# Setup of a fused attention and feed-forward kernel: early load of one bias, reordered setup work, and q_stack transfers split differently between SyncE and ScalarE

## What is computed

```python
xn = layernorm(x)
# attention block ("cosformer"): 16 heads of 16, causal, linear in L
q, k, v = split(rmsnorm(xn, n1) @ qkv_w + qkv_b)
q, k = relu(q), relu(k)                      # then times cos and sin of the position
context = q_cos * cumsum(k_cos x v) + q_sin * cumsum(k_sin x v)
norm    = q_cos . cumsum(k_cos) + q_sin . cumsum(k_sin)
h = xn + (context / (norm + 1e-6)) @ out_w + out_b
a = h + gelu(rmsnorm(h, n2) @ mlp_w1 + mlp_b1) @ mlp_w2 + mlp_b2
# second block: ternary weights, each row scaled by the mean of its absolute values
t = ternary(w_fc)    # clip(round(w / s), -1, 1) * s, s = mean(abs(w))
g = xn @ t.T + gate * (xn @ v.T @ fast_b.T @ u.T)
f = square(relu(g)) @ ternary(w_proj).T
out = x + a + f
```

## Time and profile before

| what | value |
|---|---|
| median of 3 runs | 640.94 us (640.76 to 641.73) |
| profiled execution, its own time | 644.8 us |
| its span, first to last instruction | 641.9 us |
| busy: PE, VectorE, ACT, POOL | 92%, 66%, 57%, 34% of the span |
| PE busy in the first four of 40 slices (16 us each) | 2, 7, 5, 7 tenths |
| PE busy in nearly all later slices | 9 tenths or more |

### The profile page before, as it was taken

One profiled execution on the slowest core, in us unless ns is written; L12 is line 12 of the kernel. 1 busy time (PEld: TensorE's weight loads), 2 busy tenths in 40 slices (PEclk: granted clock), 3 DMA queues, 4 the chain that ended last, 5 costly groups with the idle time before them and its releaser, 6 DMA issues.

```text
span 641.9 us, 14501 instructions
## 1 busy us (share of the span) xinstructions
PE 589.1 (92%) x5070; PEld 515.2 (80%) x5070; DVE 421.8 (66%) x776; ACT 367.5 (57%) x654; POOL 217.9 (34%) x219
## 2 busy tenths in 40 slices
PE   2757999989999999999999999999999999999986
PEld 2646878978888888888889887888879888888876
DVE  7689966477655766477664876558674786647542
ACT  5465583546745566465845657455754658455643
POOL 6006333153233432153432432334420533333220
PEclk9969999989999999999999999999999999999999
DMA  7771005600065002620056000740036200540000
GB/s 205 213 188 49 17 1 128 137 2 19 1 150 113 16 0 66 121 74 16 0 122 113 26 16 14 148 100 16 0 90 106 65 16 0 135 94 2 2 1 33
DMA packets 27992, 42.01 MB, mean 65 GB/s; under 512 B 9008, under 2 KB 19904, under 8 KB 27968
## 3 DMA queue, kind: packets, MB, share of 16 engines
q1 hardware_dynamic: 26528, 39.59, 26.7%
q10 hardware_dynamic: 1440, 2.10, 1.2%
HBM read 12.31 MB, written 4.19 MB: 26 GB/s over the span
## 4 chain that ended last, share of the span: by engine, by line
PE 78%; DVE 8%; ACT 6%; issue 2%; SPq 2%; ACTq 1%; DMA 1%; POOL 0%; DVEq 0%
PE accum L1194 20%; PE dense L1179 8%; PE dense L1356 8%; PE shared L1217 5%; DVE wide_lo L945 5%; PE ctx_ps L1242 5%; PE dense L1229 4%; PE dense L1090 4%; PE dense L1361 4%; PE shared L1330 4%; PE shared L1104 3%; PE ctx_ps L1253 2%; PE dense L1094 2%; PE dense L1184 2%; PE upd_ps L1267 2%
## 5 line engine op out<-in xcount | busy, mean ns | idle before, releaser
L945 DVE TENSOR_TENSOR wide_lo<-wide,wide_hi 128x512 fp32r<-128x512 f32 x128 | 116.7, 913 | 81.3 <-ACT wide_hi L672 74.4
L484 POOL TENSOR_TENSOR arena<-arena,tab 128x256 f32<-128x256 f32 x64 | 50.1, 804 | 142.3 <-DMA q_stack<-arena 142.3
L953 DVE TENSOR_TENSOR weighted<-shared,cst 128x512 f32<-128x512 f32 x128 | 82.8, 683 | 18.1 <-PE shared L1217 17.9
L669 ACT ACTIVATE wide<-dense,b 128x512 f32<-128x512 f32 x64 | 44.1, 690 | 80.6 <-PE dense L1361 80.2
L510 POOL TENSOR_TENSOR state<-state,added 128x544 f32<-128x544 f32 x32 | 43.6, 1363 | 115.5 <-DVE added L975 115.5
L1194 PE MATMUL accum<-w_hi,wide_hi 128*128 128x256 f32 x256 | 73.5, 287 | 8.0 <-DVE wide_lo L945 8.0
L1194 PE MATMUL accum<-prT,wide_hi 128*128 128x256 f32 x256 | 66.7, 287 | 6.8 <-DVE wide_lo L945 6.8
L1194 PE MATMUL accum<-w_lo,wide_hi 128*128 128x256 f32 x256 | 71.9, 281 | 0.0
L1194 PE MATMUL accum<-w_hi,wide_lo 128*128 128x256 f32 x256 | 71.8, 280 | 0.0
L659 ACT ACTIVATE wide<-dense,scales 128x512 f32<-128x512 f32 x64 | 44.1, 689 | 43.4 <-PE dense L1184 35.4
L1194 PE MATMUL accum<-prT,wide_lo 128*128 128x256 f32 x256 | 65.2, 281 | 0.0
(11 more groups left out here) (166 smaller groups left out, 1438.5 us busy)
## 6 DMA issues: line engine op xcount, KB each, us to landing
k_stack<-weighted SPq DMA_DIRECT2D x96, 128.0 KB, 2.7
q_stack<-arena SPq DMA_DIRECT2D x184, 64.0 KB, 2.3
xin<-L_attn_x SPq DMA_DIRECT2D x16, 256.0 KB, 2.9
out<-late SPq DMA_DIRECT2D x16, 256.0 KB, 2.3
tab<-trig SPq DMA_DIRECT2D x8, 258.0 KB, 2.7
arena<-L_ffn_w_fc SPq DMA_DIRECT2D x1, 1024.0 KB, 8.5
late<-L_ffn_w_proj SPq DMA_DIRECT2D x1, 1024.0 KB, 7.0
late<-L_attn_mlp_w ACTq DMA_DIRECT2D x1, 1024.0 KB, 5.5
```

The costliest lines, as they stand in the source:

```text
L484: pool.tensor_tensor(q_trig[:, j % 2, r, :, :], qT[:, :, k * P:(k + 1) * P], row.broadcast_to([P, KE, P]), ALU.mult).then_inc(q_trig_done, 1)
L669: act.activation(wide[:, m % 2, :], dense[m % 2][:, :], ACT.Gelu_apprx_tanh, bias=b1[:, m:m + 1]).then_inc(dense_free, 1)
L945: dve.tensor_tensor(wide_lo[:, n % 2, :], wide[:, n % 2, :], wide_hi[:, n % 2, :].bitcast(F32), ALU.subtract).then_inc(lo_done, 1)
L953: dve.tensor_tensor(weighted[:, g, :].rearrange("p (a n) -> p a n", a=4), shared[g % 2][:, :].rearrange("p (a n) -> p a n", a=4), mask.rea ...
```

## The change

It does seven things, all in the setup:

1. `qkb` is loaded right behind the constants on a semaphore of its own, `in_qkb`; the first relu waits for that and no longer for `in_small`. N_SMALL goes from 8 to 7.
2. The seven other small loads are issued behind `raw_pr`.
3. VectorE clears three quarters of `k_stack`, POOL the last quarter; `stack_zero` counts to 4.
4. PE makes `zw` behind the two k blocks; ACT reads it behind the second relu, VectorE makes its low part behind the second `k_part`.
5. VectorE splits out_w and normalises x of tile 0 right behind `x_lo`.
6. SP issues 20 of the 24 first `q_stack` transfers, ACT four (g = 3).
7. ACT issues its four between the second and the third read of `fcT`.

```diff
...
 N_Q_HI = 8
-N_SMALL = 8
+N_SMALL = 7
 
...
                              "in_const"))
+        in_qkb = sem("in_qkb")
         in_w1 = [sem(f"in_w1_{k}") for k in range(KE)]
...
             sp.dma_start(cst[:, :], consts).then_inc(in_const, 16)
+            sp.dma_start(qkb[:, :], qkv_b[0:2 * E].rearrange("(k p) -> p k", p=P),
+                         allow_slow_non_contiguous=True).then_inc(in_qkb, 16)
             sp.dma_start(v_raw, v).then_inc(in_fb, 16)
...
             smalls = [
-                (qkb[:, :], qkv_b[0:2 * E].rearrange("(k p) -> p k", p=P)),
                 (n2w[:, :], norm2_w.rearrange("(k p) -> p k", p=P)),
...
             assert len(smalls) == N_SMALL
+            sp.dma_start(raw_pr, w_proj.rearrange("(m p) n -> p m n", p=P)).then_inc(in_pr, 16)
             for dst, src in smalls:
                 sp.dma_start(dst, src, allow_slow_non_contiguous=True).then_inc(in_small, 16)
-            sp.dma_start(raw_pr, w_proj.rearrange("(m p) n -> p m n", p=P)).then_inc(in_pr, 16)
             load_tab(0)
...
                     stack_q(sp, g, 1, 1, q_lo_stacked)
-                for g in range(2 if isinstance(t, int) and t == 0 else 4):
+                for g in range(3 if isinstance(t, int) and t == 0 else 4):
                     for slot in (0, 2):
...
 
-            sp.wait_ge(stack_zero, 3)
+            sp.wait_ge(stack_zero, 4)
             stack(0)
...
 
+            pool.memset(k_stack[:, 3:4, :, :].rearrange("p g m n -> p (g m n)").bitcast(F32), 0.0).then_inc(stack_zero, 1)
             pool.memset(q_stack[:, 0:2, :, :, :].rearrange("p g r m n -> p (g r m n)").bitcast(F32),
...
 
-            act.wait_ge(zw_full, 1)
-            act.activation(zw[:, :, :].rearrange("p k n -> p (k n)"), upd_ps[:, 0:KE * P], ACT.Copy).then_inc(zw_done, 1)
             act.wait_ge(in_fc, 16)
...
                 sum_abs_fc(m)
-            act.wait_ge(in_small, 16 * N_SMALL)
+            act.wait_ge(in_qkb, 16)
             relu_block(0, 0)
...
                 sum_abs_fc(m)
-            for i in range(1, 2 * KE):
+            relu_block(0, 1)
+            act.wait_ge(zw_full, 1)
+            act.activation(zw[:, :, :].rearrange("p k n -> p (k n)"), upd_ps[:, 0:KE * P], ACT.Copy).then_inc(zw_done, 1)
+            for i in range(KE, 2 * KE):
                 relu_block(0, i)
...
             act.wait_ge(q_parts_done, 2 * KE)
-            act.wait_ge(stack_zero, 3)
-            for g in range(2, 4):
-                for slot in (0, 2):
-                    stack_q(act, g, slot, 0, q_hi_stacked[g // 2])
-
+            act.wait_ge(stack_zero, 4)
             for g in range(2):
...
                     read(SET_FC + g * KE + m, fcT[:, m, g * TOK:(g + 1) * TOK], (dense, accum)[m][g][:, :])
+                if g == 0:
+                    for slot in (0, 2):
+                        stack_q(act, 3, slot, 0, q_hi_stacked[1])
 
...
 
-            dve.memset(k_stack[:, :, :, :].rearrange("p g m n -> p (g m n)").bitcast(F32), 0.0).then_inc(stack_zero, 1)
+            dve.memset(k_stack[:, 0:3, :, :].rearrange("p g m n -> p (g m n)").bitcast(F32), 0.0).then_inc(stack_zero, 1)
             ln_statistics(0, range(NB))
...
 
-            dve.wait_ge(zw_done, 1)
-            lo_part = zw[:, :, 96:128]
-            dve.tensor_tensor(lo_part, upd_ps[:, 0:KE * P].rearrange("p (k n) -> p k n", k=KE)[:, :, 96:128],
-                              lo_part.bitcast(F32), ALU.subtract).then_inc(zw_done, 1)
+            split_weight(raw_wo, in_wo, wo_hi, wo_lo, wo_split)
+            dve.wait_ge(wo_split, 2)
+            layernorm(0)
             n = 0
...
             k_part(0, 1)
+            dve.wait_ge(zw_done, 1)
+            lo_part = zw[:, :, 96:128]
+            dve.tensor_tensor(lo_part, upd_ps[:, 0:KE * P].rearrange("p (k n) -> p k n", k=KE)[:, :, 96:128],
+                              lo_part.bitcast(F32), ALU.subtract).then_inc(zw_done, 1)
             fc_less(0)
...
 
-            split_weight(raw_wo, in_wo, wo_hi, wo_lo, wo_split)
-            dve.wait_ge(wo_split, 2)
-            layernorm(0)
             for k in range(KE):
...
             turn_x(0)
+            pe.wait_ge(qkv_split, KE + 2)
+            make_kq(0, 0)
             pe.wait_ge(fb_done, 1)
...
             mm.then_inc(zw_full, 1)
-            pe.wait_ge(qkv_split, KE + 2)
-            make_kq(0, 0)
             make_kq(0, 1)
```

## The result

The changed kernel took **643.56 us** (median of 15 executions, 642.32 to 647.43), the kernel before beside it 641.73 us (15 executions, 640.72 to 644.1). The ratio is **1.0038, 95% interval [1.0019, 1.0056]**: slower, where 638.3 us and "faster" were forecast. The profiled execution of the changed kernel took 642.93 us, its span is 640.4.

The account below looks back on a forecast made before the run. The prediction took the setup's chain of waits ahead of tile 0 as the bound, ending in POOL's start behind SP's transfers; -3.3 us there became -2.6 after POOL met VectorE: 640.94 - 2.6 = 638.3 us, range 635.6 to 640.2.

Parts of the forecast that it names:

- Relu 0: ACT's first relu in the setup: starts at 15.9 behind PE's block and not at 19.25, -3.35 us.
- out_w split and normalised x: VectorE work moved into its idle gap before the relu: fc comparisons start at 20.5 and not 23.28, -2.8 us.
- the zw products: PE in the setup: their 1.22 us leave its path, and the first kq block starts at 13.1.
- Clearing k_stack: Start of setup: a quarter moves from VectorE to POOL, and x scaled, x turned and xT come 0.4 us sooner.
- qkb early: Setup loads: qkb ahead delays w_fc and out_w by 1.2 us, to 13.9 and 14.6, with nothing lost at w_fc.
- SP takes 20 q transfers: SP's queue: 0.63 us per issue, ending at 40.9; last landing 43.2, so POOL starts 3.3 us earlier.
- C: Rival, chance 0.13: SP's queue becomes the bound at 0.73 us per transfer, issue ending at 43.7; no change.
- D: Rival, chance 0.05: SP's queue at 0.84 us per transfer, issue ending at 47.2; slower, 643.3 to 645.2 us.
- PE's clock there: PE turning prT: the second eight transposes may stay at the lower clock, 0 to +0.9 us; 0.9 taken.
- rival B: Chance 0.12: gain eaten before tile 0 by qkb's cost or PE's low clock in its matmuls; -1.2 to -1.9 us.
- POOL against VectorE: Start of tile 0: first products meet w1_lo, +0.9 us; split(0) ends behind POOL's addition; shift -2.6 us taken.
- Rival A: Chance 0.18: in tile 0 split(0) starts before POOL's addition, taking 0.7 us, not 2.74; -4.6 us in all.

Follow-up runs that it names:

- e9: The changed kernel timed again without any edit, beside the kernel before: 644.25 us, ratio 1.0024.
- e2: The changed kernel with eight q_stack transfers on ACT instead of four, behind its first two fcT reads: 639.28 us, ratio 0.9955.
- e11: e2 with the early bias undone: qkb again among eight small loads, all awaited by the first relu, w_proj behind them: 641.90 us, ratio 0.9993.
- e4: The changed kernel with w2's 1 MB load issued by SP behind its q transfers instead of by ACT: 640.97 us, ratio 0.9991.
- e5: e4 with PE's eight u4 transposes held back until VectorE's diagonals are done: 641.65 us, ratio 0.9986.
- e3: The changed kernel with 56 additional matmuls, results unread, in PE's waits: 642.13 us, ratio 0.9997.
- e14: e5 timed again without any edit: 640.59 us, ratio 0.9969.
- e12: e2 with 55 additional matmuls, results unread, in PE's waits: 638.04 us, ratio 0.9930.
- e15: e4 with 56 additional matmuls, results unread, in PE's waits, second timing of that kernel: 637.47 us, ratio 0.9933.
- e16: e2 timed again without any edit: 637.88 us, ratio 0.9938.

## Why the prediction was wrong, step by step

*Relu 0, out_w split and normalised x, the zw products*: right. Relu 0 at 16.71 (16.48 in e9) and not 15.9, the fc comparisons at 20.87 and not 20.5, -2.4 for the -2.8; prT's turn at 38.20 for **38.0**. e2 beside e11 shows what the early bias is worth in it: 0.4 to 0.6%.

*Clearing k_stack*: a miss without weight. POOL's first power comes at 8.13 and not at 7.84 or sooner. VectorE did start its statistics 0.75 us sooner (4.31), but two small operations in them then met POOL's clearing of q_stack, which the added quarter had put off to 3.83:

```profile
3.83 3.51 POOL L472 MEMSET q_stack<- 128x4096 f32 x1
...
6.18 1.18 DVE L758 TENSOR_SCALAR mean<-mean_sum 128x4 f32<-128x4 f32 x1
```

The VectorE operation and its neighbour take 1.18 and 1.12 us, where before both took 0.16 behind the end of the clearing (6.45), and they end within 0.03 us of its end (7.34). That VectorE waited for POOL there is read from these ends; no run tries it. x is scaled at 9.96 and 9.47 against 9.48 and 9.85, no gain for the 0.4.

*qkb early*: the charge of 1.2 us was about right, and cost nothing. w_fc landed at 13.7 and not 12.7, out_w at 14.4 and not 13.4. The time is lost at the issue, timeline of SP:

```profile
4.31 1.33 SPq L375 DMA_DIRECT2D added<-L_ffn_fast_b  x1
5.68 0.65 SPq L376 DMA_DIRECT2D arena<-L_ffn_w_fc  x1
```

The issue of fast_b, two places behind qkb's, takes 1.33 us (0.42 before), and w_fc's starts at 5.68 and not at 4.22; from issue to landing w_fc and out_w take 8.0 us each (8.5 and 8.1 in the earlier trace rows). Neither was waited for: ACT begins its sums of w_fc at 14.65 behind the second xT_hi, VectorE the split of out_w at 15.40 behind x_lo. The rule that the prediction took from the Trainium skill (DMA: Bandwidth & Descriptors, Rules for kernel authors) is one descriptor per element; no run counts descriptors, but qkb's 512 numbers took 6.2 us to land.

**SP takes 20 q transfers** is the step that failed. POOL was to start 3.3 us earlier, at 43.2, and started 2.1 us later, at 48.61; the 5.4 us between are two terms of that step.

- The issue, 2.9 us: its end came at 43.8 and not 40.9. The start is 0.56 later than forecast. The rate of 0.63 us was taken from a steady tile, where the setup's own rows stood beside it (8.10 for 12 and 11.25 for 16 in the earlier trace rows, 0.69 each); now 32 take 22.87 us, 0.715 each. Some 1.3 us of that is the one issue of 1.93.
- The landing, 2.5 us: 43.2 stood 2.3 us behind the end of issue, and 4.8 were measured. "w2's load no longer follows as closely" was reckoned from an issue that ends at 40.9. prT's turn, behind which w2's load is issued, came as forecast; the issue ended 2.9 us late. So the order of the two turned round, and the load came down on the last three transfers. In e4, with that load behind them, the landing takes 1.9.

Of the rivals C and D described this queue. C's condition (0.73 us an issue, an end at 43.7) was met nearly to the letter, at 0.715 and 43.78, and D's (over 0.77) was not. And yet the time is D's (643.3 to 645.2), because both rivals, like the forecast, let the last transfer land 1.7 to 3.7 us behind the end of issue. With the issue as measured and a landing of 2.3, POOL would have started at 46.1: C, no change, and e4 (45.76) is just that.

*PE's clock there*: mis-sized, though not decisive. The charge was at most 0.9, and 1 us more in rival B, where the low clock lasts through the first tile's matmuls, as it did. From prT's turn to the first scores took 8.2 us (38.20 to 46.39) against 6.4 in e2 and 5.6 in e5 (37.87 to 43.45), so up to 2.6 us. The step looked only at the idle time before prT and not at where u4's turn would go. e3 and e5 show that in tile 0 it cost nothing, since POOL and PE then wait for the queue.

*POOL against VectorE*: the mechanism is right, in every kernel: "from here the shift is POOL's". In e2, where POOL starts as forecast, this step comes out too: the first two products take 2.50 us (1.83 + 0.9 forecast), the addition over xn runs from 45.63 (45.9), and split(0) is held until 48.56, 0.6 us behind it. In the changed kernel +2.1 in place of **-3.3** gives a loss, and tile 0's output is 1.2 to 1.6 us later. Rival A's flip at split(0) came true there and was worth nothing, since two other subtractions were caught.

That what tile 0 gains or loses stays to the end holds on average only: from tile 0's output to the end of the span 514.8 to 518.2 us passed, and two executions of one kernel differ in it by up to 1.9 (e5 and e14). The first profiles of the two kernels show how far that goes: the changed kernel's span is the shorter one (640.4 against 641.9), though its tile 0 ends later. What makes the difference in the later tiles no run tells.

The fastest kernels are e12, e15 and e16 (638.0, 637.5 and 637.9 us, 0.6 to 0.7% faster than before); e16 needs no idle matmuls.

## What to carry to other kernels

When transfers are moved from one queue to another, price the last landing and not only the issue, and list every large transfer whose issue time the same change moves: here one came forward by 2.1 us, the queue's end went back by 0.9, and their order turned round. Take an issue rate from the stage in question, however good the steady loop looks. And before a cost on one engine is charged (a lower clock, say), look for what the next joint step waits for: 2.6 us on PE were free as long as POOL came later still.
